# A two-layer post-norm transformer: decoding the looked-up weights in nine chunks laid out by feed-forward tile

## The chip, the core and the metric

The kernel runs on one core of a Trainium2 chip. That core has a matmul engine (TensorE, PE in the rows), a vector engine (VectorE, DVE), an activation engine (ScalarE, ACT), a general engine (GpSimd, POOL) and a queue engine (SyncE, SP) that here issues every DMA. The metric is the time of one execution in microseconds of device time.

## The reference, cut to what matters

Four sequences of 256 tokens with 256 features pass through two layers. Each layer is attention, add, layer norm, gated feed-forward, add, layer norm. Layer 0 has 32 query heads and 8 key heads and a feed-forward of 768 whose weights are rounded to 8-bit floats. Layer 1 has 16 query heads and 8 key heads and a feed-forward of 688 whose weights are looked up: every weight is an index into a table of 16 values.

```python
def _ghost_linear(x, idx, lut):
    w = lut[idx]                                   # 16 entries
    return jnp.einsum('bsh,oh->bso', x, w)
gate = _ghost_linear(x, gate_idx, lut)             # 688 x 256
up = _ghost_linear(x, up_idx, lut)                 # 688 x 256
h = jax.nn.silu(gate) * up
return _ghost_linear(h, down_idx, lut)             # 256 x 688
```

In the kernel's layout the looked-up weights are 4,288 columns of 128 partitions: 2 x 2 x 688 = 2,752 for gate and up, 6 x 256 = 1,536 for down.

## The kernel before, in words

**Jobs.** One job is one sequence in one layer. Jobs 0 to 3 are layer 0, jobs 4 to 7 layer 1. A job has these steps, with the names of the tables: `q`, `kv` (projections, L1140, L1160, L1165), `qstack`, `kstack` (DMAs that stack three bf16 parts of queries and keys, L555, L562), `max` (matmuls L1188 into `MM`, row maxima on the vector engine L988 in layer 0 and L992 in layer 1), `mt` (the maxima turned and added to the stacks), `score` (matmuls L1218 or L1223 into `SC`, exponential on the activation engine L869), `pv` (probabilities times values, L1244), `turn`, `back`, `wo` (division, output projection, L1256, L1264, L1273, layer norm L960), `tr` (the normed rows turned, L1282), `gu` (gate and up in six tiles of 128 rows, the last of 48 in layer 1, L1301, L1060, L1063), `hsplit`, `down` (L1330, in the last job L1320).

**Order.** Every engine walks through a list of steps that is written out in a table (`ORDER`), and waits at each for semaphores. Engines do not reorder. In a `max` step of layer 0 the matmul engine may fill one half of `MM` only once the vector engine has reduced what stood there (`max_red`), so the two advance together.

**Decoding the looked-up weights.** The columns are decoded in chunks of `LUT_W` = 432, ten of them, one after the other, between the steps of jobs 0 to 3:

- `ldix` loads the indices of a chunk (SP), `lutix` casts them to bytes (ACT, L906), `lutbits` makes four masks, one per index bit (DVE, L1088).
- `lut1` picks between neighbouring table entries by the lowest bit, for eight pairs: eight instructions that write `LV[:, 0..7, :]`. In chunks 0 to 5 four of them run on POOL (L753) and four on ACT (L916), later all on POOL.
- `lut2`, `lut3`, `lut4` halve the eight candidates to four, two and one (DVE, L1104, three copies under a mask of 4, 2 and 1 times the chunk's width).
- `lutlow` on ACT (L923) writes the result, rounded for the matmul, to `W1`; `lutlow` on POOL (L742) writes what the rounding lost to `LO`; `lutlow` on SP (L613) stores that in a DRAM scratch `dw`.

The lost parts are used from `W1L`, whose memory is the same as that of `LV` and of the index buffer `IX`. So they are only loaded back (`reload`, SP, L619) when all ten chunks are decoded. The first `gu` of layer 1 (`gu.4.0.0`) waits for all chunks and for the reloaded gate and up columns, the first `down` of layer 1 for the rest.

Of the kernel before, what the change touches and what calls it, by code (L numbers as in the profile page):

```python
# [1386 lines left out]
```

## Time and profile before

| | |
|---|---|
| time, median of 3 runs | 336.48 us (332.85 to 337.21) |
| time of the profiled execution | 333.81 us |
| span of the profiled execution | 331.6 us |
| busy: PE, DVE, ACT, POOL | 300.7, 255.1, 234.9, 199.4 us |
| mean granted clock of TensorE | 0.943 |

The span is what the profile shows from the first to the last instruction; the time of the same execution has 2.2 us around it. Busy time of the matmul engine is partly modelled, since matmuls are pipelined: 91% says that something was in its pipe, not that it ran at its peak. How much of a stretch it truly needed is read from the spacing of its pieces in the chain of waits.

### The profile page before, as it was taken

To read this page: it belongs to the slowest core of one execution; us is meant where nothing else is said; L and a number is where in the kernel's file an instruction comes from. 1 tells how busy PE (TensorE), PEld (TensorE's weight loads), DVE (VectorE), ACT (ScalarE), POOL (GpSimd) and SP (SyncE) were. 2 spreads that over 40 slices of the span, in tenths; PEclk is the share of its full clock that TensorE was granted. 3 is DMA by queue.
4 is the path that set the end of the run, shared out by engine and by line. 5 is a ranking of instruction groups with operands and counts; after the bars stand their busy time and mean duration, and the time that the engine had idled before them with its cause. 6 is when DMAs were issued, how large, how long until landed. Compare 5 with 4: busy or idle time off the path is not lost.

```text
span 331.6 us, 7198 instructions
## 1 busy us (share of the span) xinstructions
PE 300.7 (91%) x2608; PEld 208.8 (63%) x2608; DVE 255.1 (77%) x472; ACT 234.9 (71%) x432; POOL 199.4 (60%) x273
## 2 busy tenths in 40 slices
PE   8555877879899999999999999999999999999993
PEld 7331333324444557678666776877879778879992
DVE  7699998999999999999985987577666744535253
ACT  2768689999997768776967966886685656564340
POOL 5876443562448489696887675655564322847664
PEclk9895768599799999999999999999999999999997
DMA  4563442153302054100320050364041000000001
GB/s 134 142 190 116 130 123 74 54 140 86 112 6 65 19 138 125 36 29 3 82 65 5 16 144 14 107 191 148 3 107 38 2 1 4 32 3 32 2 2 63
DMA packets 24889, 23.07 MB, mean 70 GB/s; under 512 B 3558, under 2 KB 24854, under 8 KB 24854
## 3 DMA queue, kind: packets, MB, share of 16 engines
q1 hardware_dynamic: 24854, 22.61, 23.7%
q8 instruction: 21, 0.34, 0.4%
q14 instruction: 14, 0.11, 0.1%
HBM read 10.47 MB, written 3.26 MB: 41 GB/s over the span
## 4 chain that ended last, share of the span: by engine, by line
PE 69%; DVE 20%; issue 5%; POOL 3%; ACT 1%; POOLq 0%; DVEq 0%; ACTq 0%
PE FB L1301 17%; PE PV L1244 12%; PE MM L1188 9%; PE FB L1330 8%; DVE MX L988 8%; DVE LV L1104 6%; PE SC L1223 4%; PE FB L1273 4%; PE SC L1218 4%; PE FB L1140 3%; PE FB L1256 2%; POOL LV L753 2%; PE FB L1282 2%; DVE QS L941 1%; PE MM L1320 1%
## 5 line engine op out<-in xcount | busy, mean ns | idle before, releaser
L869 ACT ACTIVATE PB<-SC 128x1024 f32<-128x1024 f32 x96 | 98.0, 1021 | 27.8 <-PE SC L1218 14.6
L988 DVE TENSOR_REDUCE MX<-MM 128x2 f32<-128x512 f32 x128 | 81.0, 681 | 4.8 <-PE MM L1188 3.9
L1188 PE MATMUL MM<-KS,QS 62*128 62x256 bf16 (+1 forms) x384 | 58.9, 287 | 15.0 <-DVE MX L988 11.9
L992 DVE TENSOR_REDUCE MX<-MM 128x4 f32<-128x1024 f32 x32 | 39.1, 1221 | 21.9 <-PE MM L1188 21.9
L1244 PE MATMUL PV<-PB,VP 128*32 128x256 f32 x768 | 52.8, 401 | 0.0
L735 POOL TENSOR_TENSOR HL<-HF,HH 128x256 fp32r<-128x256 f32 (+1 forms) x48 | 36.5, 771 | 24.6 <-ACT HH L846 24.5
L1188 PEld LDWEIGHTS MM<-KS,QS 62*128 62x128 bf16 (+1 forms) x384 | 24.4, 97 | 42.6 <-DVE MX L988 28.1
L1104 DVE COPY_PREDICATED LV<-LB,LV 128x1728 f32<-128x1728 uint8 (+2 forms) x30 | 41.2, 1373 | 3.5 <-POOL LV L753 3.1
L1301 PE MATMUL FB<-XH,W 128*128 128x256 f32 x192 | 43.0, 305 | 0.0
L753 POOL TENSOR_SCALAR LV<-LB,LD,LT 128x432 f32<-128x432 uint8 x56 | 38.8, 706 | 1.6 <-DVE LB L1088 0.7
L1301 PE MATMUL FB<-XL,W 128*128 128x256 f32 x192 | 38.5, 282 | 0.0
L1060 DVE SCALAR_TENSOR_TENSOR AA<-TH,FB 128x256 f32<-128x256 f32 (+1 forms) x48 | 19.9, 415 | 23.7 <-ACT TH L860 15.3
L1301 PEld LDWEIGHTS FB<-XH,W 128*128 128x128 f32 x192 | 30.2, 189 | 5.7 <-issue 4.2
L1244 PEld LDWEIGHTS PV<-PB,VP 128*32 128x32 f32 x768 | 21.3, 112 | 19.1 <-issue 9.3
L1218 PE MATMUL SC<-QS,KS 64*128 64x256 bf16 x256 | 28.4, 285 | 2.9 <-ACT PB L869 2.8
L1301 PEld LDWEIGHTS FB<-XL,W 128*128 128x128 f32 x192 | 29.5, 189 | 0.1
L846 ACT ACTIVATE HH<-HF 128x256 fp32r<-128x256 f32 (+1 forms) x48 | 19.2, 412 | 6.0 <-DVE HF L1063 5.6
L717 POOL TENSOR_TENSOR X<-X,WF 128x512 f32<-128x512 f32 x8 | 10.5, 1317 | 18.9 <-ACT WF L831 18.9
L691 POOL TENSOR_SCALAR W<-TH 128x384 fp32r<-128x384 f32 x12 | 6.9, 576 | 24.3 <-DVE TH L1080 24.3
L1218 PEld LDWEIGHTS SC<-QS,KS 64*128 64x128 bf16 x256 | 10.0, 96 | 18.0 <-ACT PB L869 9.1
L1140 PE MATMUL FB<-XT,WQ 128*128 128x256 f32 x64 | 20.4, 458 | 0.0
L696 POOL TENSOR_TENSOR QR<-QR,QP 128x512 f32<-128x512 f32 x8 | 12.6, 1580 | 11.0 <-ACT QR L773 11.0
(108 smaller groups left out, 597.4 us busy)
## 6 DMA issues: line engine op xcount, KB each, us to landing
QS<-QP SPq DMA_DIRECT2D x48, 128.0 KB, 2.4
IX<-in_idx SPq DMA_DIRECT2D x10, 216.0 KB, 3.3
dw<-LO SPq DMA_DIRECT2D x10, 216.0 KB, 2.2
W1L<-dw SPq DMA_DIRECT2D x10, 216.0 KB, 2.8
KS<-KP SPq DMA_DIRECT2D x24, 64.0 KB, 2.0
XT<-in_xt SPq DMA_DIRECT2D x4, 256.0 KB, 3.1
X<-in_x SPq DMA_DIRECT2D x4, 256.0 KB, 3.0
KS<-KP SPq DMA_DIRECT2D x24, 32.0 KB, 1.9
```

The costliest lines, as they stand in the source:

```text
L735: pool.tensor_tensor(HL[0:r, i, :], HF[0:r, c % 2, :], HH[0:r, i, :].bitcast(F32), ALU.subtract).then_inc(h_parts, 1)
L753: ins = pool.tensor_scalar(LV[:, i, :], LB[:, 0, :], LD[:, i:i + 1], LT[:, 2 * i:2 * i + 1], ALU.mult, ALU.add)
L869: act.activation(PB[:, quad % PB_QUADS, kt, :, :], SC[:, :, :], ACT.Exp, scale=DH[layer(j)] ** -0.5).then_inc(exp_done, 1)
L988: dve.tensor_reduce(mx[:, f, :], MM[:, 2 * f:2 * f + 2, :], axis=AX.X, op=ALU.max).then_inc(max_red, 1)
L992: dve.tensor_reduce(mx, MM[:, :, :].rearrange("p (f i) s -> p f i s", f=2), axis=AX.X, op=ALU.max).then_inc(max_red, 2)
L1104: ins = dve.copy_predicated(LV[:, 0:LUT // 2:2 * gap, :], mask, LV[:, gap:LUT // 2:2 * gap, :])
L1140: ins = pe.matmul(bank[:, m * S:(m + 1) * S], WQ[l][:, t, m:D:2], XT[:, b, t, :], start=t == 0, stop=t == DT - 1)
L1188: ins = pe.matmul(MM[:, 2 * f + i, :], QS[lo:lo + r, j % NST, qs + h, qt * P:(qt + 1) * P], keys(j)[lo:lo + r, j % NST, ks, :], start=True ...
L1218: ins = pe.matmul(SC[:, place(j, c), :], keys(j)[lo:lo + r, j % NST, ks, kt * P:(kt + 1) * P], QS[lo:lo + r, j % NST, qs + u % 4, :], star ...
L1244: ins = pe.matmul(PV[32 * c:32 * c + 32, r % 2, :], v, PB[:, quad % PB_QUADS, kt, place(j, c), :], start=part == 0, stop=part == (3, 1)[la ...
L1301: ins = pe.matmul(bank[:, w * S:(w + 1) * S], ffn_up(l, w, t, i)[part], xs[:, t, :], start=k == 0, stop=k == len(products) - 1)
L1330: ins = pe.matmul(bank[:, t * D:(t + 1) * D], hs[0:rows(l, i), i, t * P:(t + 1) * P], ffn_down(l, i)[part], start=i + k + t == 0, stop=(i, ...
```

## The change: nine chunks by tile, and reloads freed one by one

The columns of `W1` are laid out anew: first the 1,536 of down (chunks 0 to 2), then for each of the six feed-forward tiles its gate and up columns together (512 a tile, 192 in the last, chunks 3 to 8). `LUT_W` becomes 512, so there are eight chunks of 512 and one of 192. The indices of a gate and up chunk are loaded in four pieces of 512 B a partition, since their source keeps its layout.

A reload of chunk c overwrites `LV[:, c, :]`, and now waits only until the last chunk's decoding has read that part: odd c after `lut2.8`, c = 2 and 6 after `lut3.8`, 4 after `lut4.8`, 0 after the last `lutlow`. The last chunk's lost part is written by POOL straight into `W1L`, without scratch and reload. Each `gu` step of job 4 waits for its own chunk, each second `down` step for its own.

The last gate and up tile multiplies with 48 columns of weights instead of 128. And all five order tables are written anew.

```diff
-LUT_W = 432
+LUT_W = 512
 W1_USED = 2 * DT * I1 + 6 * D
 N_LUT = -(-W1_USED // LUT_W)
-W1_COLS = N_LUT * LUT_W
+W1_COLS = W1_USED
+W1_GU = 6 * D
+N_DW = 8
 LUT_ACT = (0, 1, 2, 3, 4, 5)
-N_LUT_GU = -(-2 * DT * I1 // LUT_W)
...
-            o = which * DT * (I0, I1)[l] + dt * (I0, I1)[l] + i * P
-            return (W0[:, o:o + P],) if l == 0 else (W1[:, o:o + P], W1L[:, o:o + P])
+            r = rows(l, i)
+            if l == 0:
+                o = which * DT * I0 + dt * I0 + i * P
+                return (W0[:, o:o + P],)
+            o = W1_GU + 2 * DT * P * i + (which * DT + dt) * r
+            return (W1[:, o:o + r], W1L[:, o:o + r])
...
                     c = step[1]
-                    sp.wait_ge(dw_wr, 16 * N_LUT)
-                    at = slice(c * LUT_W, (c + 1) * LUT_W)
-                    sp.dma_start(W1L[:, at].bitcast(F32), dw[:, at]).then_inc(low_in[c >= N_LUT_GU], 16)
+                    sp.wait_ge(dw_wr, 16 * (c + 1))
+                    if c % 2:
+                        sp.wait_ge(lut_tail, 1)
+                    elif c % 4:
+                        sp.wait_ge(lut_tail, 2)
+                    elif c:
+                        sp.wait_ge(level4, N_LUT)
+                    else:
+                        sp.wait_ge(low_done, N_LUT)
+                    sp.dma_start(W1L[:, lut_cols(c)].bitcast(F32), dw[:, lut_cols(c)]).then_inc(low_in[c], 16)
...
-                    pool.tensor_tensor(LO[:, :], LV[:, 0, :], W1[:, c * LUT_W:(c + 1) * LUT_W].bitcast(F32),
+                    low = LO[:, :] if c < N_DW else W1L[:, lut_cols(c)]
+                    pool.tensor_tensor(low, LV[:, 0, 0:lut_width(c)], W1[:, lut_cols(c)].bitcast(F32),
                                        ALU.subtract).then_inc(low_done, 1)
...
-                        elif j == first(1):
-                            pe.wait_ge(lut_done, N_LUT)
-                            pe.wait_ge(low_in[0], 16 * N_LUT_GU)
-
+                    if j == first(1) and w == 0:
+                        pe.wait_ge(lut_done, lut_chunk(i) + 1)
...
+                        if j == first(1) and w == 0 and (part, t) == (1, 0):
+                            if lut_chunk(i) < N_DW:
+                                pe.wait_ge(low_in[lut_chunk(i)], 16)
+                            else:
+                                pe.wait_ge(low_done, N_LUT)
-                        ins = pe.matmul(bank[:, w * S:(w + 1) * S], ffn_up(l, w, t, i)[part], xs[:, t, :],
+                        ins = pe.matmul(bank[0:rows(l, i), w * S:(w + 1) * S], ffn_up(l, w, t, i)[part], xs[:, t, :],
...
-        "lutbits.0 scales lut2.0 lut3.0 lut4.0 q8.0 lutbits.1 max.0.0 max.0.1 max.0.2 max.0.3 q8.1 max.0.4 lut2.1 q8.2 "
+        "scales lutbits.0 lut2.0 q8.0 lut3.0 lut4.0 max.0.0 max.0.1 lutbits.1 max.0.2 max.0.3 max.0.4 max.0.5 lut2.1 "
```

In the tables the vector engine keeps, up to `mt.2.1` (the end of the maxima of job 2), the same set of steps: the masked copies of chunks 0 to 6 and the masks of chunks 0 to 7. On PE the steps ahead of the last maxima of job 2 (`max.2.15`) are the same, and two more: `pv.2.0.1` and `tr.1.0`.

At two places the tables read as follows. The first is the start on POOL, from the first subtraction for the queries (`QR`) and the keys (`KR`) on; `LV` is `lut1.0`, `KP` the third part of the keys, `QP` that of the queries. Before:

```order
L696 TENSOR_TENSOR QR<-QR,QP 128x512
L701 TENSOR_TENSOR KR<-KR,KP 64x256
L753 TENSOR_SCALAR LV<-LB,LD,LT 128x432 x4
L662 TENSOR_TENSOR QP<-QR,QP 128x512
L666 TENSOR_TENSOR KP<-KR,KP 64x256
```

And with the change:

```order
L729 TENSOR_TENSOR QR<-QR,QP 128x512 [waits fill_free1]
L734 TENSOR_TENSOR KR<-KR,KP 64x256 [waits fill_free0]
L787 TENSOR_SCALAR LV<-LB,LD,LT 128x512 [waits bit_done,lut_steps]
L787 TENSOR_SCALAR LV<-LB,LD,LT 128x512
L699 TENSOR_TENSOR KP<-KR,KP 64x256 [waits k_mid]
L787 TENSOR_SCALAR LV<-LB,LD,LT 128x512 [waits bit_done]
L787 TENSOR_SCALAR LV<-LB,LD,LT 128x512
L695 TENSOR_TENSOR QP<-QR,QP 128x512 [waits q_mid]
```

The keys' third part now stands between the two halves of `lut1.0`.

The second place is the vector engine's list from `mt.2.1` (`MS<-MX`) on, with chunk 7 (the copies under a mask, `LV<-LB,LV`) between the maxima of job 3 (`MX<-MM`). Before:

```order
L1004 TENSOR_SCALAR MS<-MX 128x4x8
L1006 SCALAR_TENSOR_TENSOR MS<-MX,MS 128x4x8
L988 TENSOR_REDUCE MX<-MM 128x2 x2
L1104 COPY_PREDICATED LV<-LB,LV 128x4x432
L988 TENSOR_REDUCE MX<-MM 128x2 x2
L1104 COPY_PREDICATED LV<-LB,LV 128x2x432
L1104 COPY_PREDICATED LV<-LB,LV 128x432
L988 TENSOR_REDUCE MX<-MM 128x2 x2
L1088 TENSOR_TENSOR LB<-IB,BITS 128x432
```

And with the change:

```order
L1038 TENSOR_SCALAR MS<-MX 128x4x8
L1040 SCALAR_TENSOR_TENSOR MS<-MX,MS 128x4x8
L1022 TENSOR_REDUCE MX<-MM 128x2 x2
L1140 COPY_PREDICATED LV<-LB,LV 128x4x512
L1022 TENSOR_REDUCE MX<-MM 128x2 x2
L1140 COPY_PREDICATED LV<-LB,LV 128x2x512
L1140 COPY_PREDICATED LV<-LB,LV 128x512
L1022 TENSOR_REDUCE MX<-MM 128x2 x2
L1094 SCALAR_TENSOR_TENSOR AA<-TH,FB 128x256
```

Chunk 7 stands at the same place, 80 columns wider; the masks of the next chunk have moved behind.

## Rows read from the trace of the kernel before

**Rows 1.** Busy time by stage: stretch, its length, engines, granted clock, DMA share, GB/s.

```profile
0.00:22.10 22.10, 14.28 (x60) 11.05 (x60) 16.65 (x24) 10.39 (x21) 14.34 (x19) 0.92 0.49 138
22.10:57.50 35.40, 25.35 (x142) 10.30 (x138) 33.40 (x57) 29.57 (x61) 17.27 (x23) 0.71 0.42 127
57.50:96.10 38.60, 33.14 (x293) 14.38 (x293) 36.44 (x58) 36.73 (x63) 17.86 (x23) 0.87 0.30 85
96.10:131.50 35.40, 33.63 (x345) 19.86 (x348) 34.31 (x68) 27.50 (x45) 26.79 (x38) 1.00 0.29 82
131.50:172.50 41.00, 41.00 (x428) 28.01 (x421) 38.08 (x73) 30.80 (x55) 32.51 (x40) 1.00 0.16 43
172.50:325.70 153.20, 153.20 (x1352) 125.21 (x1350) 93.24 (x185) 99.93 (x192) 88.79 (x127) 1.00 0.16 46
```

**Rows 2.** Chain of waits, around its change from DVE to PE, and later.

```profile
122.58 0.48 DVE HF L1063
123.06 1.21 DVE MX L988 x2
...
124.92 1.62 PE FB L1301 x12
...
236.94 0.92 PE FB L1160 x4
...
246.81 2.83 PE FB L1301 x24
...
301.85 4.26 PE FB L1301 x36
```

**Rows 3.** What DVE waited for, 22.1 to 131.5: total us, times, longest.

```profile
DVE MX L988 <- PE MM L1188: 2.3, 4, 1.3
DVE LV L1104 <- POOL LV L753: 0.5, 1, 0.5
```

**Rows 4.** Timeline of DVE: start, us, instruction: masked copies of four, two, one width; masks.

```profile
30.00 2.06 DVE L1104 COPY_PREDICATED LV<-LB,LV 128x1728 f32<-128x1728 uint8 x1
...
34.01 1.13 DVE L1104 COPY_PREDICATED LV<-LB,LV 128x864 f32<-128x864 uint8 x1
...
38.54 0.63 DVE L1104 COPY_PREDICATED LV<-LB,LV 128x432 f32<-128x432 uint8 x1
...
40.09 0.59 DVE L1088 TENSOR_TENSOR LB<-IB,BITS 128x432 int32<-128x432 int32 x1
```

**Rows 5.** Busy time by stage of the masked copies (L1104) alone.

```profile
22.10:57.50 35.40, 7.64 (x6) 0.71 0.42 127
57.50:96.10 38.60, 11.05 (x8) 0.87 0.30 85
96.10:131.50 35.40, 4.54 (x4) 1.00 0.29 82
131.50:172.50 41.00, 7.87 (x6) 1.00 0.16 43
172.50:200.00 27.50, 4.98 (x3) 1.00 0.20 54
```

**Rows 6.** Timeline of POOL at the start.

```profile
12.20 0.66 POOL L701 TENSOR_TENSOR KR<-KR,KP 64x256 f32<-64x256 f32 x1
13.52 2.75 POOL L753 TENSOR_SCALAR LV<-LB,LD,LT 128x432 f32<-128x432 uint8 x4 [0.66 <-DVE LD L1067]
16.24 1.15 POOL L662 TENSOR_TENSOR QP<-QR,QP 128x512 bf16<-128x512 f32 x1
17.35 2.50 POOL L666 TENSOR_TENSOR KP<-KR,KP 64x256 bf16<-64x256 f32 x1
```

**Rows 7.** Timeline of DVE, first decoding; of PE, first max.

```profile
16.31 5.19 DVE L1104 COPY_PREDICATED LV<-LB,LV 128x1728 f32<-128x1728 uint8 x3 [2.60 <-POOL LV L753]
...
21.86 0.40 PE L1188 MATMUL MM<-KS,QS 62*128 62x256 bf16 x4 [2.51 <-DMA KS<-KP]
```

**Rows 8.** Groups of ACT instructions by shape: busy us, mean ns, idle before.

```profile
L797 ACT ACTIVATE QP<-QR 128x512 bf16<-128x512 f32 x8 | 5.0, 628 | 1.3 <-POOL QR L696 1.3
...
L923 ACT ACTIVATE W<-LV 128x432 fp32r<-128x432 f32 x10 | 5.6, 558 | 3.4 <-DVE LV L1104 3.4
```

**Rows 9.** DMA issues: KB each, median us from issue to landing.

```profile
IX<-in_idx SPq DMA_DIRECT2D x10, 216.0 KB, 3.3
W1L<-dw SPq DMA_DIRECT2D x10, 216.0 KB, 2.8
KS<-KP SPq DMA_DIRECT2D x24, 64.0 KB, 2.0
```

More of the change, by code:

```diff
@@ L339, in two_layer_kernel @@
         W1L = sb("W1L", [P, W1_COLS], F32R)
+        sb("IX_END", [P, 10 * LUT_W - W1_COLS])
         LT = sb("LT", [P, LUT])
@@ L433, in two_layer_kernel @@
         dw_wr = sem("dw_wr")
-        low_in = [sem(f"low_in{i}") for i in range(2)]
+        low_in = [sem(f"low_in{i}") for i in range(N_DW)]
+        lut_tail = sem("lut_tail")
         ib_done = sem("ib_done")
@@ L497, in rows, with lut_cols, lut_width, lut_chunk @@
             return min(P, (I0, I1)[l] - i * P)
+        def lut_cols(c):
+            return slice(c * LUT_W, min((c + 1) * LUT_W, W1_COLS))
+        def lut_width(c):
+            return min(LUT_W, W1_COLS - c * LUT_W)
+        def lut_chunk(i):
+            return (W1_GU + 2 * DT * P * i) // LUT_W
         def stacked(j, g):
@@ L538, in load_idx @@
             def load_idx(c):
-                sp.dma_start(IX[:, c % 2, :], idx[:, c * LUT_W:(c + 1) * LUT_W]).then_inc(ld_idx[c % 2], 16)
+                if c < lut_chunk(0):
+                    o = 2 * DT * I1 + c * LUT_W
+                    sp.dma_start(IX[:, c % 2, :], idx[:, o:o + LUT_W]).then_inc(ld_idx[c % 2], 16)
+                else:
+                    i = c - lut_chunk(0)
+                    r = rows(1, i)
+                    sp.dma_start(IX[:, c % 2, 0:2 * DT * r].rearrange("p (k n) -> p k n", k=2 * DT),
+                                 idx[:, 0:2 * DT * I1].rearrange("p (k n) -> p k n", k=2 * DT)[:, :, i * P:i * P + r]
+                                 ).then_inc(ld_idx[c % 2], 16)
             for step in order("SP"):
@@ L905, in _ @@
                         act.wait_ge(bit_done, c)
-                    act.activation(IB[:, :], IX[:, c % 2, :], ACT.Copy).then_inc(ib_done, 1)
+                    act.activation(IB[:, 0:lut_width(c)], IX[:, c % 2, 0:lut_width(c)], ACT.Copy).then_inc(ib_done, 1)
                 elif kind == "lut1":
@@ L915, in _ @@
                     for i in range(2 * part, 2 * part + 2):
-                        ins = act.activation(LV[:, i, :], LB[:, 0, :], ACT.Identity, scale=LD[:, i:i + 1],
+                        ins = act.activation(LV[:, i, 0:lut_width(c)], LB[:, 0, 0:lut_width(c)], ACT.Identity, scale=LD[:, i:i + 1],
                                              bias=LT[:, 2 * i:2 * i + 1])
@@ L922, in _ @@
                     act.wait_ge(level4, c + 1)
-                    act.activation(W1[:, c * LUT_W:(c + 1) * LUT_W], LV[:, 0, :], ACT.Copy).then_inc(lut_done, 1)
+                    act.activation(W1[:, lut_cols(c)], LV[:, 0, 0:lut_width(c)], ACT.Copy).then_inc(lut_done, 1)
         @block.vector
@@ L1086, in _ @@
                     src = IB[:, :].bitcast(I32)
[L1087 to L1089 removed]
+                    w = lut_width(c) // 4
+                    bits = LB[:, :, :].rearrange("p k w -> p (k w)").bitcast(I32).rearrange("p (k w) -> p k w", k=4)
+                    dve.tensor_tensor(bits[:, :, 0:w],
+                                      src.rearrange("p (o w) -> p o w", o=1)[:, :, 0:w].broadcast_to((P, 4, w)),
                                       BITS[:, :].rearrange("p (k o) -> p k o", o=1).broadcast_to((P, 4, w)),
@@ L1102, in _ @@
                     pairs = LUT // 4 // gap
-                    mask = LB[:, k:k + 1, :].broadcast_to((P, pairs, LUT_W)) if pairs > 1 else LB[:, k:k + 1, :]
-                    ins = dve.copy_predicated(LV[:, 0:LUT // 2:2 * gap, :], mask, LV[:, gap:LUT // 2:2 * gap, :])
+                    w = lut_width(c)
+                    mask = LB[:, k:k + 1, 0:w].broadcast_to((P, pairs, w)) if pairs > 1 else LB[:, k:k + 1, 0:w]
+                    ins = dve.copy_predicated(LV[:, 0:LUT // 2:2 * gap, 0:w], mask, LV[:, gap:LUT // 2:2 * gap, 0:w])
                     if k == 3:
                         ins.then_inc(level4, 1)
+                    elif c == N_LUT - 1:
+                        ins.then_inc(lut_tail, 1)
+                        dve.wait_ge(lut_tail, k)
                     else:
@@ L1308, in _ @@
                     pe.wait_ge(h_hi, 6 * j + i + 1)
-                    if j == first(1) and i == 0:
-                        pe.wait_ge(low_in[1], 16 * (N_LUT - N_LUT_GU))
+                    if j == first(1) and i % 2 == 0:
+                        pe.wait_ge(low_in[i // 2], 16)
                     products = ((0, HH), (1, HH))[:1 + l] + ((0, HL),)
```

12 lines of the change are left out of this document (5 added, 7 removed), and 231 rows, old and new, of the table ORDER.

## The prediction, written before the change was run

> **What bounds the kernel now.** I read the busy time by stage first. The reader is to see two regimes [rows 1]. From 131.5 us to 325.7 us PE is busy all the time, 41.00 of 41.00 and 153.20 of 153.20 us, at a granted clock of 1.00. From 22.1 to 131.5 us (109.4 us) it is DVE that is full: 33.40 + 36.44 + 34.31 = 104.2 us busy, 5.3 us idle, while ACT is nearly full between 57.5 and 96.1 us (36.73 of 38.60).
>
> The chain of waits says the same and gives the place of the hand-over: its last DVE piece of any weight is the maxima at 123.06 us, and from 124.9 us on it holds PE pieces only, until 325.7 us [rows 2]. Matmuls stand there back to back (36 in 4.26 us, 118 ns each), so no wait of another engine can be shortened in the last 200 us. The time is therefore **the moment at which DVE lets PE go, plus PE work that is the same before and after**, unless the change gives PE more to do ahead of that moment.
>
> DVE's idle time is the third thing to look at: of the 5.3 us, waits for another engine are 2.3 us on the max matmuls and 0.5 us on POOL's `lut1` [rows 3], with some smaller ones about 3.2 us; the rest is the gaps between dependent instructions.
>
> **The change part by part.** *The wider chunks on DVE.* A masked copy takes 2.06 us at 1,728 elements and 1.13 us at 864 [rows 4], so 1.08 ns an element and 0.2 us fixed. 80 columns more, times 4 + 2 + 1, are 560 elements: 0.60 us a chunk. Up to the hand-over DVE's list holds the same steps as before, among them the copies of chunks 0 to 6 (before: 3 at 16.3 us [rows 7] and 6 + 8 + 4 by 131.5 us [rows 5]) and eight masks. Seven chunks cost 7 x 0.60 = 4.2 us. The masks, 0.59 us for 432 columns [rows 4], get 80 columns wider: at the copies' rate 0.085 us each, 0.7 us for eight; in proportion it would be 0.9. Together **+4.9 us** ahead of the hand-over, in a stage where DVE is 95% busy.
>
> *What the wider chunks save.* A chunk fewer and 32 columns fewer save three copies of 0.2 us fixed and a mask. But the saved work lies where chunk 9 ran, after 172.5 us (4.98 us [rows 5]), when DVE is busy 93.24 of 153.20 us and PE sets the pace [rows 1]: worth 0. Without that cover it would give at most those 5 us.
>
> The rows show a fixed part of 0.2 us a copy. The Trainium skill ("VectorE: DVE Perf Modes", section on the TRN2 errata) says the same and draws the advice to work on 512 elements or more, so that the fixed part weighs less. By that rule alone the change would save under 1 us of DVE time and lose none; the rows by stage go against using it here, since the total falls while the share ahead of the hand-over rises.
>
> *The start on POOL.* The first copies began at 16.31 us, after 2.60 us of waiting for POOL's `lut1.0` [rows 7]. Now the keys' third part is put between its two halves. The same shape took 0.66 us undisturbed and 2.50 us beside DVE's copies [rows 6]; here no copy runs yet, so I take 0.66. The four POOL instructions (2.75 us, 0.69 each [rows 6]) widen by at most 80/432, 0.5 us together; I take 0.4. So **+1.1 us**, bounds 0.7 and 3.0. The first max matmuls waited for the stack of the keys (21.86 us, [rows 7]); now the query's third part comes last, and the last stack DMA would be issued near 21 us and land about 2 us later [rows 9], near 23 us. DVE reaches its first maximum only near 24 us, so this costs 0; if POOL is held as long as at 17.35 us (2.50 for 0.66, 1.8 us more), it costs about 1 us.
>
> That long POOL instruction lies wholly beside the masked copies of chunk 0, which are themselves slow there (5.19 us for what is later 3.8) [rows 5 to 7]. The Trainium skill ("SBUF — State Buffer", section Who interferes with whom) has a rule for it: a DVE instruction with two inputs in SBUF and a GpSimd instruction that reads SBUF block each other for a whole instruction. By that rule wider copies hold POOL longer each time, and the sum would be 1.8 us longer, at 340.1 us.
>
> *DVE's idle time.* PE and POOL get more time between DVE's maxima, and POOL's list now puts the query subtraction of job 2 behind `lut1.3`, for which DVE waited 0.5 us [rows 3]. Of the 3.2 us of named waits I take half as regained, **-1.5 us**; bounds 0 and -5.3, all of DVE's idle time.
>
> *PE's list.* Ahead of `max.2.15` it holds two steps more (a `pv` and a `tr`), well under 1 us of work; at `max.3.0` five `pv` steps have taken the place of two of `down`. I count 0, bounds 0 and -0.7.
>
> *Reloads and their waits.* In job 4 the matmuls of the first tile began at 246.81 us [rows 2] with no gap ahead, so reloading was hidden before and earlier reloads gain 0. Do the late ones come too late? Reloads 4 and 0 stand on SP behind the key stack of job 7, whose projection began at 236.94 us [rows 2]; with 2.8 us to land [rows 9] they have some 7 us in hand, and the down weights of chunk 0 more. Reload 0 makes SP wait for POOL's last `lutlow`, with job 7's stacks queued behind it; that is a subtraction of 192 columns, under 1 us, and those stacks are used after 250 us. Cost 0; without that cover, 3 us.
>
> *Index loads in 512 B pieces.* Key stacks move in such pieces, 64 KB in 2.0 us; 216 KB of long pieces take 3.3 us [rows 9]. The loads run chunks ahead: 0, at worst some us at a place with tens in hand.
>
> *The last gate and up tile* (48 matmuls with 48 weight columns). Each still streams 256 columns; at best 118 ns [rows 2] become some 110: 0.4 us. I count 0. ACT's wider work (below) I count at 0 too, as long as DVE is behind it.
>
> **Sum.** 333.81 (the profiled execution, span 331.6) + 4.9 + 1.1 - 1.5 = **338.3 us**. That execution is 2.7 us under the median of the three runs (336.48), inside their spread (332.85 to 337.21). Two per cent, 6.7 us, is about what a measurement of this kernel can tell from no change: 329.8 and 343.2 us around the median.
>
> **The rivals.** *A: DVE's idle time swallows it; not slower.* The place is 22 to 131.5 us. If every microsecond of idle time went, 333.81 + 4.9 + 1.1 - 5.3 = 334.5 us. It decides if DVE's idle time in that stage falls from 5.3 to about 1 us. For it: about 3.2 us are waits on PE and POOL, who get more time. Against it: the gaps between dependent copies stay, and ACT and PE have little to spare. Chance 0.2.
>
> *B: ACT becomes a second bound; slower.* An ACT instruction of 512 columns took 628 ns, of 432 columns 558 [rows 8]: 0.07 us more. Chunks 0 to 5 have six on ACT each: 6 x 6 x 0.07 = 2.5 us, in a stage where ACT is 95% busy [rows 1]. If it comes on top of DVE's, and nothing is regained, and POOL is held 1.8 us at the start, the time is 333.81 + 4.9 + 1.1 + 2.5 + 1.8 = 344.1 us. It decides if ACT's idle time from 57.5 to 96.1 us goes to zero while DVE's grows. Chance 0.22.
>
> *C: faster by over 2%.* It would need PE to do 7 us of work more ahead of the hand-over, or DVE to do less; the lists show neither. I leave 0.05 for what I don't see, such as a late stage of PE with fewer matmul gaps than rows 1 lets me think.
>
> **How the numbers follow.** The forecast, 336.5 to 341 us, has the remaining 0.53. Its time, 338.3, is the predicted one. The range goes down to 333 us (most of rival A, and 5 us of idle regained with the PE steps) and up to 343.5 us (most of rival B). Faster by over 2%: 0.05. Slower by over 2%: most of B and the upper edge of the forecast in a comparison with a run as quick as the profiled one, 0.2. Within 2%: 0.75.
>
> **What would show it.** Right: copies of about 2.4, 1.3 and 0.7 us; the 21 copies ahead of `mt.2.1` take some 4 us more; the end of `mt.2.1` (131.5 us before) moves to 135 to 137 us, and the span by the same; from there on PE busy without a gap and the distance from `mt.2.1` to the end unchanged within 1 us; no wait of PE on a reload in job 4. Wrong: an end of `mt.2.1` at 133 us or sooner (rival A), DVE waiting more for PE or ACT than before (rival B), or a distance from `mt.2.1` to the end that has changed by more than 2 us, which would mean that PE's work after the hand-over is not the constant I take it for.

## The result, and the profile after

The changed kernel takes **344.12 us** (median of 4 runs, 342.93 to 345.87) against 336.61 us for the kernel before in the same comparison: ratio 1.030, 95% interval 1.0245 to 1.0355. That is slower, by 7.5 us, and 0.6 us above the upper end of the range. Medians here and below are over all executions, while ratios leave out those over 1.5% slower than the fastest of their kernel and so can differ from the quotient of two medians (1.022 here). The profiled execution took 342.93 us (span 341.1), 9.1 us more than the profiled execution of before.

The busy time by stage, cut as before where the last instruction of each maximum table begins (`mt.0.1` 62.5 us, `mt.1.1` 103.7, `mt.2.1` 141.6, `mt.3.1` 180.5), answers to [rows 1]. Columns as there.

```profile
0.00:22.10 22.10, 14.04 (x57) 10.40 (x58) 15.41 (x23) 10.57 (x20) 12.99 (x20) 0.85 0.53 150
22.10:62.50 40.40, 29.03 (x123) 10.94 (x122) 37.32 (x60) 30.11 (x60) 19.17 (x23) 0.50 0.44 122
62.50:103.70 41.20, 35.51 (x328) 15.79 (x324) 38.60 (x59) 38.85 (x66) 18.72 (x22) 0.87 0.26 73
103.70:141.60 37.90, 34.51 (x360) 19.26 (x358) 36.66 (x68) 28.32 (x46) 29.25 (x39) 1.00 0.27 80
141.60:180.50 38.90, 38.37 (x390) 27.08 (x391) 34.49 (x65) 29.05 (x50) 28.69 (x37) 1.00 0.14 40
180.50:335.20 154.70, 154.36 (x1362) 125.81 (x1360) 91.37 (x187) 99.25 (x192) 83.62 (x121) 1.00 0.15 42
```

The three stages in which DVE is full are longer, 40.4, 41.2 and 37.9 us for 35.4, 38.6 and 35.4. Behind them PE is full again, and the distance from the end of `mt.2.1` to the end of the span is 199.5 us for 200.1. All of the loss arises ahead of the hand-over (10.0 us at `mt.2.1`, 9.5 in the span). In the first of these stages the granted clock is 0.50 (0.71 before).

The chain of waits (start, length, piece) shows the hand-over from DVE to PE, near 129 us instead of 124.9 [rows 2]. It leaves PE again around 160 us, for POOL's `lut1` and a copy, but PE is busy 38.37 of 38.90 us there:

```profile
120.11 2.45 DVE LV L1140
122.58 1.35 DVE LV L1140
...
126.04 1.28 DVE MX L1022 x2
...
128.04 1.21 DVE MX L1022 x2
129.68 1.06 PE FB L1312 x4
...
159.67 3.90 POOL LV L787 x8
163.60 1.03 DVE LV L1140
```

What DVE waited for between 22.1 and 141.6 us (total, times, longest; [rows 3]): the maxima's matmuls, 3.6 us for 2.3.

```profile
DVE MX L1022 <- PE MM L1227: 3.6, 7, 1.4
DVE LV L1140 <- ACT LV L950: 0.4, 1, 0.4
```

DVE's groups from the first copies (16.79 us) to the end of `mt.2.1`: operation, shape, count, busy time, mean ns, idle time ahead. The copies answer to [rows 4, 5].

```profile
L1022 DVE TENSOR_REDUCE MX<-MM 128x2 f32<-128x512 f32 x97 | 62.0, 683 | 4.8 <-PE MM L1227 3.6
L1140 DVE COPY_PREDICATED LV<-LB,LV 128x2048 f32<-128x2048 uint8 x7 | 18.1, 2585 | 4.3 <-POOL LV L787 3.9 <-ACT LV L950 0.4
L1140 DVE COPY_PREDICATED LV<-LB,LV 128x1024 f32<-128x1024 uint8 x7 | 9.2, 1321 | 0.1
L1114 DVE COPY_PREDICATED TH<-BIG,HF 128x384 f32<-128x384 uint8 x12 | 8.1, 674 | 0.4
L1140 DVE COPY_PREDICATED LV<-LB,LV 128x512 f32<-128x512 uint8 x7 | 5.9, 843 | 0.1
L1123 DVE TENSOR_TENSOR LB<-IB,BITS 128x512 int32<-128x512 int32 x7 | 5.3, 760 | 0.1
```

The same groups took 61.2, 15.6, 8.2, 7.4, 4.5 and 4.2 us before, in the same order. Single copies with nothing beside them are what was forecast: 2.42, 1.28 and 0.72 us.

```profile
33.56 2.42 DVE L1140 COPY_PREDICATED LV<-LB,LV 128x2048 f32<-128x2048 uint8 x1
...
36.75 1.28 DVE L1140 COPY_PREDICATED LV<-LB,LV 128x1024 f32<-128x1024 uint8 x1
...
42.35 0.72 DVE L1140 COPY_PREDICATED LV<-LB,LV 128x512 f32<-128x512 uint8 x1
```

POOL's start (timeline, [rows 6]) went as forecast, `kv.0` in its undisturbed 0.66 us between the two halves of `lut1.0`; DVE's first copies begin at 16.79 us for 16.31 [rows 7].

```profile
13.12 1.52 POOL L787 TENSOR_SCALAR LV<-LB,LD,LT 128x512 f32<-128x512 uint8 x2 [1.36 <-DVE LB L1123]
14.60 0.66 POOL L699 TENSOR_TENSOR KP<-KR,KP 64x256 bf16<-64x256 f32 x1
15.25 1.51 POOL L787 TENSOR_SCALAR LV<-LB,LD,LT 128x512 f32<-128x512 uint8 x2
16.73 1.15 POOL L695 TENSOR_TENSOR QP<-QR,QP 128x512 bf16<-128x512 f32 x1
```

Last, two places in the timelines of DVE and of POOL where an instruction stretched: a masked copy of 384 columns, 0.59 us elsewhere, and a mask, 0.68 elsewhere, take 1.58 and 1.22 us beside subtractions on POOL.

```profile
26.25 0.68 DVE L1123 TENSOR_TENSOR LB<-IB,BITS 128x512 int32<-128x512 int32 x1
...
36.27 0.59 DVE L1114 COPY_PREDICATED TH<-BIG,HF 128x384 f32<-128x384 uint8 x1
...
109.32 1.58 DVE L1114 COPY_PREDICATED TH<-BIG,HF 128x384 f32<-128x384 uint8 x1
...
124.90 1.22 DVE L1123 TENSOR_TENSOR LB<-IB,BITS 128x512 int32<-128x512 int32 x1
```

```profile
109.19 1.27 POOL L776 TENSOR_TENSOR LO<-LV,W 128x512 f32<-128x512 f32 x1
...
124.81 0.75 POOL L768 TENSOR_TENSOR HL<-HF,HH 128x256 fp32r<-128x256 f32 x1 [6.07 <-ACT HH L880]
```

### The profile page after: what moved, and what is told of

Its sections match the earlier page's. It is cut to its first block, busy times and chain, and to the rows that moved or that the text cites. A ratio compares the mean times of both kernels' runs of the same rounds, so it can differ in the third digit from the quotient of the medians.

```text
span 341.1 us, 7183 instructions
## 1 busy us (share of the span) xinstructions
PE 306.0 (90%) x2608; PEld 209.3 (61%) x2608; DVE 256.9 (75%) x468; ACT 236.1 (69%) x430; POOL 194.3 (57%) x264
## 4 chain that ended last, share of the span: by engine, by line
PE 59%; DVE 23%; issue 6%; POOL 4%; ACT 3%; DMA 2%; SPq 1%; POOLq 0%; DVEq 0%; ACTq 0%
PE FB L1343 12%; PE PV L1283 10%; PE MM L1227 9%; DVE LV L1140 8%; DVE MX L1022 7%; PE FB L1372 7%; PE SC L1262 4%; PE FB L1312 3%; PE SC L1257 3%; PE FB L1179 2%; POOL LV L787 2%; PE FB L1295 2%; PE FB L1199 1%; PE FB L1321 1%; PE MM L1362 1%
## 5 line engine op out<-in xcount | busy, mean ns | idle before, releaser
L1227 PE MATMUL MM<-KS,QS 62*128 62x256 bf16 (+1 forms) x384 | 63.0, 300 | 14.9 <-DVE MX L1022 12.3
L1026 DVE TENSOR_REDUCE MX<-MM 128x4 f32<-128x1024 f32 x32 | 39.1, 1221 | 23.0 <-PE MM L1227 22.8
L1283 PE MATMUL PV<-PB,VP 128*32 128x256 f32 x768 | 51.7, 396 | 0.0
L1140 DVE COPY_PREDICATED LV<-LB,LV 128x2048 f32<-128x2048 uint8 (+5 forms) x27 | 40.8, 1511 | 5.3 <-POOL LV L787 4.5
L1343 PE MATMUL FB<-XH,W 128*128 128x256 f32 (+1 forms) x192 | 43.1, 306 | 0.0
L1343 PE MATMUL FB<-XL,W 128*128 128x256 f32 (+1 forms) x192 | 38.5, 282 | 0.0
L787 POOL TENSOR_SCALAR LV<-LB,LD,LT 128x512 f32<-128x512 uint8 (+1 forms) x48 | 34.1, 723 | 2.1 <-DVE LB L1123 1.4
L1343 PEld LDWEIGHTS FB<-XH,W 128*128 128x128 f32 (+1 forms) x192 | 29.6, 184 | 4.1 <-issue 2.3
L1343 PEld LDWEIGHTS FB<-XL,W 128*128 128x128 f32 (+1 forms) x192 | 29.1, 184 | 0.1
L1262 PE MATMUL SC<-QS,KS 98*128 98x512 bf16 x64 | 19.3, 382 | 0.0
L1343 PE MATMUL FB<-XH,W1L 128*128 128x256 f32 (+1 forms) x96 | 19.2, 281 | 0.0
```

The lines of the kernel that those rows point to most:

```text
L787: ins = pool.tensor_scalar(LV[:, i, 0:lut_width(c)], LB[:, 0, 0:lut_width(c)], LD[:, i:i + 1], LT[:, 2 * i:2 * i + 1], ALU.mult, ALU.add)
L1026: dve.tensor_reduce(mx, MM[:, :, :].rearrange("p (f i) s -> p f i s", f=2), axis=AX.X, op=ALU.max).then_inc(max_red, 2)
L1140: ins = dve.copy_predicated(LV[:, 0:LUT // 2:2 * gap, 0:w], mask, LV[:, gap:LUT // 2:2 * gap, 0:w])
L1227: ins = pe.matmul(MM[:, 2 * f + i, :], QS[lo:lo + r, j % NST, qs + h, qt * P:(qt + 1) * P], keys(j)[lo:lo + r, j % NST, ks, :], start=True ...
L1262: ins = pe.matmul(SC[:, 2 * f:2 * f + 2, :], keys(j)[lo:lo + r, j % NST, ks, kt * P:(kt + 1) * P], QS[lo:lo + r, j % NST, qs:qs + 2, :], s ...
L1283: ins = pe.matmul(PV[32 * c:32 * c + 32, r % 2, :], v, PB[:, quad % PB_QUADS, kt, place(j, c), :], start=part == 0, stop=part == (3, 1)[la ...
```

## The experiments

Three theories were put to the test. **Width**: the wider chunks put more work on DVE ahead of the hand-over, and each microsecond of it counts. **Order**: the new order tables cost half of the loss by themselves. **Rival B** of the prediction: ACT (or POOL), whose part of the decoding is wider too, holds DVE. The table has the ratio to the kernel before of each run's own comparison; tables `mt` are from one profiled execution each, which need not lie at the median. Before: 57.5 and 131.5 us; changed: 62.5 and 141.6.

| run | width, order | median us | ratio (95%) | `mt.0.1` | `mt.2.1` |
|---|---|---|---|---|---|
| e1 | 480, old | 339.1 | 1.0108 (1.0068–1.0148) | 57.8 | 134.2 |
| e2 | copies 432, new | 341.4 | 1.0113 (1.0004–1.0221) | 61.2 | 140.4 |
| e3 | 512, old | 343.4 | 1.0234 (1.0153–1.0314) | 59.0 | 142.7 |
| e4 | 432, one chunk later | 345.0 | 1.0267 (1.0195–1.0340) | 59.4 | 133.4 |
| e5 | all 432, new | 337.8 | 1.0095 (1.0056–1.0134) | 60.3 | 136.1 |
| e6 | all 432, old | 335.5 | 0.9987 (0.9945–1.0029) | 59.6 | 133.8 |
| e7 | 512, old start, new rest | 340.9 | 1.0182 (1.0117–1.0246) | 58.8 | 138.2 |
| e8 | 512, new, warm early | 344.3 | 1.0287 (1.0211–1.0363) | 62.8 | 141.6 |
| e9 | DVE 432, new | 338.8 | 1.0141 (1.0081–1.0200) | 61.3 | 136.7 |
| e10 | ACT and POOL 432, new | 342.2 | 1.0245 (1.0186–1.0303) | 62.0 | 140.9 |
| e11 | 392, old | 341.0 | 1.0220 (1.0153–1.0286) | 55.0 | 127.3 |
| e12 | 392, placed | 335.2 | 0.9987 (0.9938–1.0035) | 59.7 | 132.1 |
| e13 | 392, placed later | 334.5 | 0.9955 (0.9913–0.9998) | 56.5 | 128.9 |
| e14 | 512, new, one load later | 345.1 | 1.0301 (1.0239–1.0363) | 62.4 | 144.1 |
| e15 | 512, new, `q.2.0` later | 343.5 | 1.0239 (1.0180–1.0299) | 61.0 | 139.6 |
| e16 | 512, new, warm later | 343.6 | 1.0257 (1.0173–1.0341) | 63.6 | 142.1 |

### Width and order apart: e1, e3, e6, e5

e1, in the code of before:

```diff
-LUT_W = 432
+LUT_W = 480
 # order of before without the steps of chunk 9
```

> Width alone: the code of before with chunks of 480 columns instead of 432, in the order tables of before without the steps of the chunk that is no longer there. Seven chunks are decoded ahead of the end of the sixth maximum table (131.5 us before, 141.6 us after), each 48 columns wider, 0.6 of the widening of the change. Theory W (width explains the whole of the 10 us that VectorE ends later, part of it as waits): 0.6 of 10 us, so the table ends near 137.5 us and the run takes about 342.6. Theory O (the new order tables cost about half): only the width's own VectorE work counts, 0.6 of 5.4 us = 3.3, so the table ends near 134.8 us and the run takes about 339.9. ScalarE as the bound (rival B of the prediction): VectorE's waits for TensorE and GpSimd grow by more than 3 us over those of before, with its own work up by 3.3.

Measured: 3.8 us more in the medians (339.1 to 335.3), `mt.2.1` at 134.2. This is the forecast in which the width's own work on DVE counts, once, without waits on top: DVE's busy time from the first copies to that table is 114.9 us for 110.0, its idle time 3.8 for 5.4, and the copies begin at 15.66 us for 16.31. So it came out partly by luck: the work grew by 4.9 us, not 3.3, and less idle time and an earlier start took 2.3 of it back. The profiled execution (337.0 us) is 2.1 us under its median.

e3: the code of the change in the order of before (steps of chunk 9 left out).

> The code of the change (nine chunks of 512, its layout and its reload waits) in the order tables of before, without the steps of the tenth chunk. Theory W (width explains all): as the changed kernel, the sixth maximum table ends near 141.6 us and the run takes about 344. Theory O (the new tables cost 4 to 5 of the 10 us): the table ends near 137 us, the run takes about 341.5 at most, and the stretch to the end of the second table ends near 59.5 us instead of 62.5.

Measured: 343.4 us, `mt.2.1` at 142.7. With the old order the width costs as much as the whole change. Theory Order, as it was put, falls; only its forecast for the second table (59.0 instead of 62.5 us) came true, and that gain was gone by `mt.2.0` (124.5 and 124.8 us).

e5 and e6 take the width out on every engine and leave the layout, the loads and the reload waits of the change:

```diff
 def lut_width(c):
-    return min(LUT_W, W1_COLS - c * LUT_W)
+    return min(432, W1_COLS - c * LUT_W)
```

> The changed kernel in its own order tables, with the decode work of every engine 432 columns wide in a chunk of 512 (index conversion, masks, first level, masked copies; the two steps that store the result stay at full width, and columns 432 to 511 of each chunk hold zeros). It differs from the run with narrow masked copies alone, 341.4 us, in ScalarE's, GpSimd's and the masks' width. If ScalarE or GpSimd held VectorE (rival B of the prediction), the rest of the loss goes too: about 336 us, sixth maximum table near 132 us. If the order tables hold the rest, with TensorE at half clock from 24 to 68 us whatever the width, the mask's 0.7 us and little more comes back: about 339.5 to 340.5 us, table near 139 us.

> As the run before it in this list (new code, every engine's decode work 432 columns wide in chunks of 512), but in the order tables of before without the steps of the tenth chunk. It has before's decode work, before's order and the change's layout, loads and reload waits. If only width and tables matter, it takes what before takes, 335 to 336.5 us, with the sixth maximum table near 131.5 us. If the layout (strided index loads, waits by chunk in the feed-forward tiles) costs something of its own, it takes over 338 us.

Measured: e6 335.5 us, not to be told from the kernel before: layout, strided loads, waits by tile and one chunk fewer are together worth nothing either way (the interval allows a gain of 1.8 us and a loss of 1.0). Its reloads stand where before had them; the change's stand elsewhere, and behind `mt.2.1` it takes 199.5 us for e6's 200.0. e5 337.8 us. So, in medians, the width costs 344.1 - 337.8 = 6.4 us in the new order and 343.4 - 335.5 = 8.0 us in the old (unrounded); the order costs 2.3 us at 432 columns and 0.7 at 512. By the ratios, each to its own comparison's kernel before, the same four are 6.9, 8.3, 3.6 and 2.2 us, so they are known to 1.5 us or so; that the width is the larger part holds either way.

### Which engine's width: e2, e9, e10

e2, in the change:

```diff
-                    w = lut_width(c)
+                    w = min(432, lut_width(c))      # masked copies only
```

> The changed kernel with VectorE's masked copies 432 columns wide instead of 512: columns 432 to 511 of each chunk are left undecided by the last three levels of the lookup, everything else is as in the change. If the masked copies count one for one, they take 4.5 to 4.9 us less ahead of the end of the sixth maximum table (141.6 us in the changed kernel), so it ends near 137 us and the run takes about 339.5. If ScalarE, GpSimd or the order of the steps holds VectorE there (rival B), the copies' time turns into waits: the table still ends at 140 to 142 us and the run takes 343 to 344.

Measured: 341.4 us, with single times from 337.1 to 342.2. The interval holds the first forecast and ends at 342.7 us, just under the second, so the run does not part them. In its profile (341.62 us) DVE is 4.6 us less busy ahead of `mt.2.1` than in the change, but its waits for the maxima's matmuls took 2.7 us of that, and the first copies began 0.9 us later:

```profile
DVE MX L1022 <- PE MM L1227: 6.3, 9, 1.5
```

e9 narrows masks and copies on DVE from chunk 1 on, e10 the index conversion and first level on ACT and POOL:

```diff
+def part_width(c):
+    return min(432 if c else LUT_W, W1_COLS - c * LUT_W)
```

> The changed kernel with VectorE's decode work alone (masks and masked copies) 432 columns wide from the second chunk on; ScalarE's and GpSimd's stay at 512 (columns 432 to 511 of these chunks are not decided by it). All engines narrow took 337.8 us, the copies alone 341.4, the change 344.1. If VectorE's work is what the width costs, this takes the loss away as far as all engines narrow did, about 338 to 339 us. If ScalarE and GpSimd carry the other half (rival B), it takes 341 us, as with narrow copies alone.

> The changed kernel with ScalarE's and GpSimd's decode work alone (index conversion, first level) 432 columns wide from the second chunk on; VectorE's masks and copies stay at 512 (columns 432 to 511 of the first level keep the first chunk's values). If ScalarE or GpSimd hold VectorE (rival B), 3 us or more of the loss goes and it takes 341 us or less; if VectorE's own work is what counts, it takes 343 to 344.5 us, and VectorE's busy time ahead of the sixth maximum table stays at 118 us.

Measured: e9 338.8 us, e10 342.2. DVE's width is 5.4 of the 7.5 us, ACT's and POOL's together 1.9, between the two forecasts, and the intervals of e10 and of the change overlap. Rival B is at most the smaller part. Nor was its sign there: ACT's idle time between `mt.0.1` and `mt.1.1` was 1.9 us before and 2.3 us after, not zero.

### The new start: e7, e14, e15, e8, e16

e7 keeps the order of before up to `mt.0.1` on each engine and the change's behind it.

> The changed kernel (512 wide) with the order tables of before up to the second maximum table on each engine, and its own order for everything behind it. The old tables reached that point at 59.0 us with the new code, the new ones at 62.5; behind it the new tables took 79.1 us to the sixth table, the old ones 83.7. If the start of the new tables costs 3.5 us of its own, the sixth table ends near 138 us and the run takes about 340.5. If what is lost at the start is lost elsewhere anyway, the table ends at 141 to 142 us and the run takes 343 to 344.

Measured: 340.9 us, `mt.2.1` at 138.2, as forecast: the start of the new tables costs 3 us. Its first copies begin at 15.82 us instead of 16.79, and DVE's idle time from there to `mt.2.1` is 4.3 us instead of 7.0, its waits for the maxima's matmuls 1.8 instead of 3.6. Its granted clock from 36 to 56 us is higher too, 0.74 for 0.50. Two runs looked for the item among the steps, and two more, e8 and e16, at the clock.

```diff
 # e14, SP, as in before:
-ldix.3 ldix.4 qstack.1.1 ... lutlow.1
+ldix.3 qstack.1.1 ... lutlow.1 ldix.4
 # e15, PE, as in before:
-max.0.2 q.2.0 max.0.3 ... max.0.6 kv.2.0
+max.0.2 max.0.3 ... max.0.6 q.2.0 kv.2.0
```

> The changed kernel with the load of the fifth chunk's indices on SyncE's queue where the order of before had it, behind the store of the second chunk; in the change it stands behind the load of the fourth, and SyncE waits 4.4 us there, from 25.0 to 29.4 us, with the stacks and weight loads of the second job behind it. The run with the old start took 340.9 us against 344.1. If SyncE's wait is what the new start costs, this run takes 341 us, second maximum table at 59 to 60 us; if not, 344 us, table at 62.5.

> The changed kernel with one query projection of the third job (2.07 us of TensorE at half clock, between maximums 2 and 3 of the first job, VectorE idle for 1.44 us behind it) moved behind maximum 6, where the order of before had it. If that is what the new start costs, the second maximum table ends 1.5 to 3 us earlier (62.5 us in the changed kernel) and the run takes 341 to 342.5; if not, 344.

Measured: e14 345.1 us, nothing gained; the 4.4 us for which SP waited cost nobody. e15 343.5 us, 0.6 less than the change, too little for its interval; in its profile the wait of 1.44 us behind `q.2.0` is gone and `mt.2.1` ends 2.0 us earlier, but that execution (340.89 us) is the fastest of its four, 2.6 us under their median. The step may be a part of the 3 us; the rest stays open.

e8 and e16 add matmuls that compute nothing, to raise the clock:

```diff
+if j == 0 and u in WARM:      # e8: {0: 4, 1: 2, 7: 3, 8: 2}
+    for _ in range(WARM[u]):  # e16: {7: 7, 8: 2, 9: 2, 12: 2, 13: 3}
+        pe.matmul(PV[:, 0, 0:P], IDN[:, :], IDN[:, :], start=True, stop=True)
```

> The changed kernel with 11 more matmuls on TensorE that compute nothing: identity by identity into the bank that the first weighted values use later, 4 ahead of maximum 0 of the first job, 2 ahead of maximum 1, 3 ahead of maximum 7, 2 ahead of maximum 8, at places where TensorE waited 2.3, 1.5, 2.6 and 0.7 us for others. They only keep TensorE at work. If the half clock from 24 to 68 us is what makes VectorE wait and the narrow copies not count, the granted clock rises in that stretch, the second maximum table ends 2 to 3 us earlier (62.5 us in the changed kernel), and the run takes about 341 to 342. If the clock stays, or if VectorE's own work is what sets the pace there, the run takes 344 or a little more.

> The changed kernel with 16 matmuls of identity by identity that compute nothing, later than in the first run of this kind: 7 ahead of maximum 7 of the first job (where TensorE waited 2.6 us), 2 ahead of maximums 8, 9 and 12, 3 ahead of maximum 13. The kernels whose granted clock rose in the stretch from 36 to 56 us (0.74 to 0.87) ended the second maximum table 3 us earlier than kernels with the same instructions whose clock stayed at 0.54 there. If the clock of that stretch is the cause, and the added matmuls raise it there, the table ends near 59.5 to 60.5 us instead of 62.5 and the run takes 341 to 342. If the clock rises and the table doesn't move, the clock is a companion and not the cause, and the run takes 344. If the clock stays at 0.50, the run says nothing on it.

Measured: 344.3 and 343.6 us. In e8 the clock rose only ahead of 28 us. In e16 it rose to 0.70 and 1.00 from 36 to 44 us (0.50 in the change), fell back to 0.55 behind that, and `mt.0.1` ended at 63.6 us, not earlier (its first copies began 0.85 us later). Busy time by stretch, columns as in [rows 1], e16 and then the change:

```profile
36.00:40.00 4.00, 3.80 (x19) 2.65 (x17) 3.90 (x6) 1.60 (x4) 2.07 (x2) 0.70 0.32 86
40.00:44.00 4.00, 3.15 (x23) 2.15 (x23) 3.86 (x11) 3.19 (x9) 1.71 (x3) 1.00 0.38 113
44.00:56.00 12.00, 8.40 (x44) 3.52 (x43) 10.73 (x15) 10.97 (x22) 5.04 (x7) 0.55 0.51 139
```

```profile
36.00:40.00 4.00, 1.39 (x5) 0.26 (x4) 3.87 (x8) 2.47 (x6) 2.06 (x2) 0.50 0.47 130
40.00:44.00 4.00, 3.29 (x16) 2.28 (x16) 3.90 (x10) 3.03 (x8) 2.00 (x3) 0.50 0.37 95
44.00:56.00 12.00, 8.08 (x39) 2.81 (x39) 11.15 (x16) 10.83 (x20) 4.76 (x6) 0.50 0.49 131
```

DVE is busy 3.9 of 4 us at either clock where the clock was raised, so it had nothing to give there. Of the 20 us from 36 to 56 us DVE is idle 1.1 in the change, most of it behind 44 us, where e16 stayed near half; what a higher clock would give of that, and of the 1.44 us ahead of 30 us that DVE waits behind `q.2.0` (2.07 us of PE at 0.50), no run shows.

### The other direction: e4, e11, e12, e13

e4 is the kernel before with chunks 6 to 9 decoded one place later, so that one chunk less lies ahead of the hand-over.

```diff
 # DVE: chunk 6 in the place of 7, 7 of 8, 8 of 9, 9 behind the fourth job's gate steps
-lut2.6 lut3.6 mt.2.0 lut4.6 ... mt.2.1 ... lut2.7
+mt.2.0 ... mt.2.1 ... lut2.6
```

> The kernel before with one thing moved: decode chunks 6 to 9 each one place later, so that VectorE decodes six chunks instead of seven ahead of the end of the sixth maximum table. If VectorE's work ahead of the hand-over to TensorE counts one for one, one chunk of copies (2.06 + 1.13 + 0.63 us and a mask of 0.59) goes: the table ends near 127 us instead of 131.5, the distance from there to the end stays 200 us, and the run takes about 332. If the work is only put off (TensorE waits later for the weights, or VectorE becomes late again behind it), the distance grows by the same 4 us and the run takes about 336.5.

Measured: 345.0 us. `mt.2.1` ends at 133.4 us; e6, which decodes that chunk there and has the same granted clock at the start (0.56 and 0.55 from 36 to 56 us), at 133.8. The work was taken away (107.1 us of DVE for 110.8) and DVE waited instead (11.1 us idle for 7.4), once for 2.6 us, for matmuls that stand behind a run of 40 `pv` matmuls in PE's list:

```profile
118.99 1.29 DVE L988 TENSOR_REDUCE MX<-MM 128x2 f32<-128x512 f32 x2 [2.62 <-PE MM L1188]
```

So at that place PE and DVE were even, and a chunk less gave nothing. Less work on every chunk did give there: e11, below, ends the same table 4.2 us earlier than before, at like clocks (0.84 and 0.78 from 36 to 56 us). The rest of the loss is chunk 9 in its new place, in the chain of waits:

```profile
222.67 2.74 POOL LV L753 x4
225.41 0.02 issue
225.44 3.29 DVE LV L1104
```

e11 is before's code with eleven chunks of 392 columns, the work spread thinner over all stages; e12 and e13 place the eleventh chunk elsewhere.

```diff
-LUT_W = 432
+LUT_W = 392
 # DVE, e11: max.5.6 lut2.10 gu.3.1 gu.3.2 lut3.10 lut4.10
 # e12:      max.5.4 lut2.10 max.5.5 lut3.10 gu.3.0 max.5.6 lut4.10
 # e13:      max.5.5 lut2.10 gu.3.0 max.5.6 lut3.10 gu.3.1 gu.3.2 lut4.10
 # POOL, e11: kdif.6 lut1.10.0 .. lut1.10.3;  e12, e13: wo.3 lut1.10.0 lut1.10.1 (the rest on ACT)
```

> The other direction: the kernel before with eleven chunks of 392 columns instead of ten of 432, in its own order, with the eleventh chunk behind the tenth (its index conversion behind the third job's feed-forward, its copies inside the fourth job's, its store and all reloads behind the twelfth maximum table). Seven chunks are 40 columns narrower ahead of the sixth maximum table. The run with chunks of 480 lost 3.6 us for 48 columns more. If the time goes with the width both ways, this one gains 3 us: about 332.5, the table near 128.5. If the kernel before stood where VectorE and TensorE are even, as the run with one chunk later suggests (TensorE became late when VectorE's work was taken away), it gains 1 us or nothing: 334.5 to 336.

> Eleven chunks of 392 columns as in the run before, with the eleventh placed where the engines idle: the tenth's store earlier (ScalarE behind the stage of the fourth job's second half, GpSimd behind the third job's down step), half of the eleventh's first level on ScalarE, the other half on GpSimd in the place of the tenth's store, its copies one by one behind maximums 4, 5 and 6 of the sixth job. The run before ended its sixth table at 127.3 us (131.5 before) and its eleventh at 206.1 (210.1), and then lost 12 us in the place of the eleventh chunk (masked copy 4.15 us beside GpSimd's work, 3.3 us of waiting for GpSimd). If that place is all that was wrong, the 4 us stay and the run takes 332 to 333.5 us, faster than both kernels. If less width doesn't shorten the end, because TensorE has no room for it, the run takes 335.5 or more.

> As the run before in this list, the eleventh chunk's copies one maximum later each (behind maximums 5 and 6 and the third gate step of the fourth job). If the place of these copies is uncritical once GpSimd is out of their way, the same time within 1 us (332 to 333.5); if they hold the twelfth table, 1 to 3 us more or less than the run before.

Measured: e11 had `mt.2.1` at 127.3 us, 4.2 earlier than before, and `mt.5.0` still 4.0 earlier; then 8 us went in the place of chunk 10 (`mt.5.0` to `mt.5.1` 22.8 us for 14.7; the 12 us in e12's expectation were a slip), where DVE waited 3.3 us for POOL and then copied beside it:

```profile
216.16 4.15 DVE L1105 COPY_PREDICATED LV<-LB,LV 128x1568 f32<-128x1568 uint8 x1 [3.33 <-POOL LV L754]
```

```profile
216.09 1.15 POOL L663 TENSOR_TENSOR QP<-QR,QP 128x512 bf16<-128x512 f32 x1
217.21 0.72 POOL L736 TENSOR_TENSOR HL<-HF,HH 128x256 fp32r<-128x256 f32 x1
```

With that chunk in idle places, e12 and e13 take 335.2 and 334.5 us. e13 is below the kernel before by 0.45% (0.02 to 0.87), less than forecast: 2.6 us were still gained at `mt.2.1`, but between `mt.5.0` and `mt.5.1` it needs 16.8 us where before needed 14.7. Nor is the 0.45% a gain at the same clock. Seven of its twelve executions had a mean granted clock of 0.941 or more and a median of 333.2 us; eight of 23 of the kernel before had 0.939 or more, with a median of 333.1 us. e13 had such executions more often.

e12 and e13 run the same instructions up to some 200 us, and in their profiled executions (337.63 and 333.73 us) DVE begins the same maximum at 40.28 us in both; then the granted clock differs (0.54 and 0.84 from 36 to 56 us). DVE's timeline of e12, then of e13:

```profile
42.81 4.07 DVE L990 TENSOR_REDUCE MX<-MM 128x2 f32<-128x512 f32 x6 [1.25 <-PE MM L1190]
...
54.53 1.29 DVE L990 TENSOR_REDUCE MX<-MM 128x2 f32<-128x512 f32 x2 [2.21 <-PE MM L1190]
```

```profile
40.28 4.90 DVE L990 TENSOR_REDUCE MX<-MM 128x2 f32<-128x512 f32 x8
...
51.27 1.29 DVE L990 TENSOR_REDUCE MX<-MM 128x2 f32<-128x512 f32 x2 [0.65 <-PE MM L1190]
```

At half clock DVE waited 3.46 us for the maxima's matmuls, at the higher one 0.65, and `mt.0.1` ends at 59.7 and 56.5 us. The kernel before and e4 run the same instructions up to some 95 us, and part in the same place, with 0.78 and 0.56 from 36 to 56 us. DVE's timeline of before, then of e4:

```profile
40.60 4.86 DVE L988 TENSOR_REDUCE MX<-MM 128x2 f32<-128x512 f32 x8
...
52.47 1.29 DVE L988 TENSOR_REDUCE MX<-MM 128x2 f32<-128x512 f32 x2 [1.26 <-PE MM L1188]
```

```profile
42.86 4.07 DVE L988 TENSOR_REDUCE MX<-MM 128x2 f32<-128x512 f32 x6 [1.20 <-PE MM L1188]
...
54.20 1.29 DVE L988 TENSOR_REDUCE MX<-MM 128x2 f32<-128x512 f32 x2 [1.53 <-PE MM L1188]
```

The query projection in front of these maxima, begun near 40 us, takes 1.14 us in before and e13 and 2.07 in e4 and e12, and `mt.0.1` ends at 57.5 us in before and 59.4 in e4. In the old order, then, the clock does make a difference of 2 to 3 us. What makes one execution get it and another not stays open.

## Why the prediction was wrong

**What held.** The frame: DVE sets the time up to the hand-over, PE behind it. `mt.2.1` moved by 10.0 us and the span by 9.5. Copies took what was forecast, alone. Index loads, the shorter last tile and the saved chunk were together worth nothing (e6), and so were the late reloads, since the distance behind `mt.2.1` stayed.

**What failed: the sizes of three terms of the sum**, +4.9 for DVE's work ahead of the hand-over, -1.5 for idle time regained, and the 333.81 us that it starts from. Two references part them. One is the profiled execution of before, from which the sum started. The other is that of e6, which has the old order and width: its 335.58 us are at its median, and its granted clock from 36 to 56 us, 0.55, is near the 0.50 of the change. DVE from the first copies to the end of `mt.2.1` (stretch, its length, busy time, granted clock, DMA share, GB/s) in before, in the change and in e6:

```profile
16.31:131.73 115.42, 110.03 (x189) 0.86 0.34 100
```

```profile
16.79:141.75 124.96, 117.97 (x189) 0.79 0.33 91
```

```profile
15.69:133.95 118.26, 110.83 (x189) 0.81 0.34 99
```

| term | forecast | change against before | change against e6 |
|---|---|---|---|
| copies of seven chunks | +4.2 | +4.9 (28.3 to 33.2) | +4.8 |
| masks (eight; seven behind the first copies) | +0.7 | +1.1 (4.2 to 5.3) | +1.1 |
| other DVE work | 0 | +1.9 (maxima +0.8, weight copies +0.7, rest +0.4) | +1.3 |
| DVE idle | -1.5 | +1.6 (5.4 to 7.0) | -0.4 (7.4 to 7.0) |
| first copies begin | +1.1 | +0.5 | +1.1 |
| sum at `mt.2.1` (terms rounded) | +4.5 | +10.0 | +7.8 |

*DVE's busy time* missed 3.0 us against before and 2.3 against e6, because undisturbed durations were multiplied. Beside POOL they don't hold: chunk 0's copies took 6.2 us for 4.4 alone (5.2 for 3.8 before), the copy at 109.32 us 1.0 more and the mask at 124.90 us 0.5 more than elsewhere. That makes some 2 of the 3 us. Of the maxima's 0.8 us, 0.3 is a longer mean (680 to 683 ns for 97); for the rest, fewer of them overlap with the one before. [Rows 5 to 7] held a pair that stretched, at the start, and the prediction kept it out of the sum. The trace agrees with the rule of the Trainium skill ("SBUF — State Buffer", Who interferes with whom), and at more places than the start.

*DVE's idle time* missed by 3.1 us against before, but by 1.1 against e6. Half of the named waits were counted as regained on the ground that PE and POOL get more time between maxima. POOL's wait at `lut1.3` did go, and the waits on PE did not: 3.6 us in the change, where `q.2.0` now stands between two maxima (1.44 us, at half clock), for 2.3 in the profiled execution of before and 3.9 in e6. e5, the new order at the old width, has 7.8 us. So the error was to read the new list for what it saves DVE and not for what it puts in its way, and to take the waits of one execution with a high clock for those of the kernel.

*The start of the sum* is the third miss. The profiled execution had the higher clock at the start (0.78 from 36 to 56 us; 0.54 to 0.56 in e4, e6 and e12 with the old order). Of the 23 executions of before beside e12 to e15, eight had a mean granted clock of 0.939 to 0.948 and took 331.8 to 333.8 us; the other fifteen had 0.918 to 0.929 and took 335.8 to 337.1 us. The profiled one, at 0.943, is of the first kind; the four of the change have 0.904 to 0.914. The prediction said that it lay 2.7 us under the median and did not count it. So some 2 to 3 of the 5.8 us between 338.3 and 344.1 come from the execution that the sum began with, and the rest from the two terms above.

**The rivals.** A is out: it needed some 1 us idle, and 7.0 were left. B named the time, 344.1, by luck: the 1.8 us of a held POOL did not come (0.66 us), and its sign, ACT's idle time gone, was not there; 1.9 us of its cause may be (e10).
